# ScalarE weights the gathered rows, VectorE builds plain one-hots, in a two-layer graph kernel

## The reference

```python
h = relu(ln(x @ W1 + b1, g1, bt1))
h_src = h[row]                                   # row = src, col = dst
ef = concatenate([h_src, h[col]], axis=1)
edge_weights = sigmoid(relu(ef @ We1 + be1) @ We2 + be2)[:, 0]
aggr = segment_sum(edge_weights[:, None] * h_src, col, num_segments=n)
gate = sigmoid(concatenate([h, aggr], axis=-1) @ Wg + bg)
h_new = gate * aggr + (1.0 - gate) * h
```

## Time and profile before

| | |
|---|---|
| median of 3 runs | 2092.99 us (2092.58 to 2093.82) |
| profiled execution, its own time | 2085.86 us |
| its span, first to last instruction | 2084.1 us |
| mean granted TensorE clock | 0.898 |

### The profile page before, as it was taken

One profiled execution on the slowest core, in us unless ns is written; L12 is line 12 of the kernel. 1 busy time (PEld: TensorE's weight loads), 2 busy tenths in 40 slices (PEclk: granted clock), 3 DMA queues, 4 the chain that ended last, 5 costly groups with the idle time before them and its releaser, 6 DMA issues.

```text
span 2084.1 us, 44754 instructions
## 1 busy us (share of the span) xinstructions
PE 1614.4 (77%) x14694; PEld 1506.6 (72%) x14695; DVE 1661.9 (80%) x4900; ACT 1087.2 (52%) x2658; POOL 1409.8 (68%) x1430
## 2 busy tenths in 40 slices
PE   4999998766777688887877787887888777787880
PEld 3788786655676677877777787877788777787750
DVE  7777886887998679887888887898797787777766
ACT  1566564676553255554565554565564444444335
POOL 4365530487677777777777777777777777777735
PEclk9999999597888689999999989999899998999995
DMA  7899998037444556655665656666566666666502
GB/s 275 282 333 318 324 366 279 11 101 244 133 140 130 158 161 180 179 175 179 174 179 168 185 175 194 192 187 189 176 205 188 188 188 188 198 176 199 145 18 62
DMA packets 278514, 392.87 MB, mean 189 GB/s; under 512 B 74753, under 2 KB 178436, under 8 KB 278155
## 3 DMA queue, kind: packets, MB, share of 16 engines
q1 hardware_dynamic: 218783, 230.00, 34.7%
q0 software_dynamic: 57024, 155.79, 25.7%
q10 hardware_dynamic: 2476, 4.22, 0.6%
HBM read 374.69 MB, written 15.12 MB: 187 GB/s over the span
## 4 chain that ended last, share of the span: by engine, by line
POOL 46%; PE 20%; issue 18%; DVE 11%; DMA 2%; DVEq 1%; ACT 1%; SPq 0%; ACTq 0%; POOLq 0%
POOL x_rows L969 28%; PE psum L521 10%; POOL ring L969 9%; POOL late_gathers L969 8%; DVE sums L1909 3%; PE psum L1342 2%; PE psum L556 1%; DVE stats L1821 1%; PE psum L1372 1%; PE psum L529 1%; DVE weighted L568 1%; PE psum L573 1%; PE psum L1313 1%; DVE ring L1833 1%; DVE psum L562 1%
## 5 line engine op out<-in xcount | busy, mean ns | idle before, releaser
L969 POOL DMA_INDIRECT x_rows<-src_table,lane_src x720 | 695.8, 966 | 226.4 <-issue 216.4
L562 DVE SCALAR_TENSOR_TENSOR psum<-psum,we_all 128x1024 f32<-128x1024 f32 (+1 forms) x273 | 270.3, 990 | 146.5 <-PE psum L556 145.9
L1179 ACT ACTIVATE weight<-logit,be_all 128x12 f32<-128x12 f32 (+2 forms) x149 | 45.2, 304 | 619.8 <-DVE logit L564 619.8
L556 PE MATMUL psum<-x_rows,ident 128*128 128x128 f32 x1440 | 225.2, 322 | 163.0 <-DMA x_rows<-src_table,lane_src 162.8
L577 DVE TENSOR_TENSOR sums<-sums,psum 128x128 f32 (+4 forms) x812 | 200.9, 247 | 172.5 <-issue 101.0
L556 PEld LDWEIGHTS psum<-x_rows,ident 128*128 128x128 f32 x1440 | 209.5, 231 | 173.0 <-issue 149.1
L564 DVE TENSOR_REDUCE logit<-psum 128x8 f32<-128x1024 f32 (+1 forms) x273 | 266.9, 977 | 20.4 <-issue 0.4
L969 POOL DMA_INDIRECT ring<-src_table,lane_src x236 | 226.8, 961 | 71.9 <-issue 71.9
L969 POOL DMA_INDIRECT late_gathers<-src_table,lane_src x232 | 221.8, 956 | 70.7 <-issue 70.7
L568 DVE TENSOR_SCALAR weighted<-iota,lane_dst,weight 128x40 f32<-128x40 f32 x1188 | 268.9, 322 | 0.0
L521 PE MATMUL psum<-ring 128*64 128x128 f32 x3128 | 221.2, 285 | 24.2 <-issue 19.1
(11 more groups left out here) (266 smaller groups left out, 3406.7 us busy)
## 6 DMA issues: line engine op xcount, KB each, us to landing
ring<-in_edge_attr SPq DMA_DIRECT2D x195, 512.0 KB, 5.4
ring<-rel_table SPq DMA_DIRECT2D x74, 512.0 KB, 5.7
ring<-cell_table SPq DMA_DIRECT2D x121, 256.0 KB
ring<-src_table SPq DMA_DIRECT2D x144, 128.0 KB
x_rows<-src_table,lane_src POOLq DMA_INDIRECT x720
ring<-dst_table SPq DMA_DIRECT2D x297, 32.0 KB
ring<-src_table SPq DMA_DIRECT2D x104, 64.0 KB
src_table<-ring SPq DMA_DIRECT2D x12, 512.0 KB, 2.9
```

Of the source, the lines that this page charges most:

```text
L556: last = eng.matmul(out[:, j, :], ident[:, :], rows_[:, j, 0:P], start=False, stop=True, skip_group_check=True)
L562: eng.scalar_tensor_tensor(hid, hid, 0.0, wide["we2"][:, :].unsqueeze(1).to_broadcast([P, n, P]), ALU.max, ALU.mult)
L969: eng.indirect_dma_start(gathered(c)[:, j, :], None, src_table, bass.IndirectOffsetOnAxis(ap=lane_src[:, t:t + 1], axis=0)).then_inc(gathe ...
```

## The change

ScalarE, behind the sigmoid, drains and multiplies each of the pair's eight gathered h rows (128 x 128 f32) in place by its edge weight; only then is `weight` signalled. VectorE's eight small instructions become one comparison of 128 x 320 elements (`tensor_tensor`, is_equal, both inputs broadcast), which no longer needs the weights and now stands ahead of the rider's instructions; these wait for `weight` where there is a rider. `wsum` waits for `weight` as well. `add_src_part` makes one identity product of 512 columns for a chunk in place of four of 128.

```diff
         def add_src_part(eng, out, rows_):
-            for j in range(J):
-                last = eng.matmul(out[:, j, :], ident[:, :], rows_[:, j, 0:P], start=False, stop=True, skip_group_check=True)
-            return last
+            return eng.matmul(out, ident[:, :], rows_[:, :, 0:P], start=False, stop=True, skip_group_check=True)
...
                 some = slice(0, n * J + (n_cols if n == 2 else 0))
-                eng.activation(weight_[:, some], logit_[:, some], ACT.Sigmoid, bias=be2_all[:, 0:1]).then_inc(done("weight"), 1)
+                eng.activation(weight_[:, some], logit_[:, some], ACT.Sigmoid, bias=be2_all[:, 0:1])
+                eng.drain()
+                for k, c in enumerate(pair_chunks(q)):
+                    for j in range(J):
+                        h_rows = gathered(c)[:, j, P:2 * P]
+                        last = eng.activation(h_rows, h_rows, ACT.Copy, scale=weight[:, q % 4, k, j:j + 1])
+                last.then_inc(done("weight"), 1)
...
             def wsum(q):
                 need(eng, "weigh", q)
+                need(eng, "weight", q)
                 need(eng, "acc2", q - 2)
...
             def weigh_(q):
-                c = SORTED + 2 * q
+                c, n = SORTED + 2 * q, len(pair_chunks(q))
                 need(eng, "wsum", q - 3)
-                need(eng, "weight", q)
+                last = eng.tensor_tensor(weighted[:, q % 3, 0:n, :, :].rearrange("p c j w -> p (c j) w"),
+                                         iota1[:, 0:W].unsqueeze(1).to_broadcast([P, n * J, W]),
+                                         lane_dst[:, c:c + n, :].rearrange("p c j -> p (c j)").unsqueeze(2).to_broadcast([P, n * J, W]), ALU.is_equal)
                 if q in riders:
+                    need(eng, "weight", q)
                     need(eng, "wsum", q - PLACES)
-                    cell_weigh(riders[q], q)
-                for k in range(len(pair_chunks(q))):
-                    last = weigh(eng, weighted[:, q % 3, k, :, :], lane_dst[:, c + k, :], weight[:, q % 4, k, :])
+                    last = cell_weigh(riders[q], q)
                 last.then_inc(done("weigh"), 1)
```

More of the change, by code:

```diff
@@ L1958, in cell_weigh @@
                 for i in range(n):
-                    eng.tensor_scalar(place_dst[u % PLACES][:, i, 0:span(u)], iota_s[:, 0:span(u)], cell[:, 1, at_.start + i:at_.start + i + 1],
-                                      weight[:, q % 4, 2, i:i + 1], ALU.is_equal, ALU.mult)
+                    last = eng.tensor_scalar(place_dst[u % PLACES][:, i, 0:span(u)], iota_s[:, 0:span(u)], cell[:, 1, at_.start + i:at_.start + i + 1],
+                                             weight[:, q % 4, 2, i:i + 1], ALU.is_equal, ALU.mult)
+                return last
             def logits(q):
```

## The result

The changed kernel takes 2106.94 us in the median of 13 runs (2097.07 to 2112.65), the kernel before 2092.99 (13 runs, 2090.86 to 2098.5): ratio 1.0065, 95% interval 1.0054 to 1.0076. It is slower by some 14 us, where I had forecast 2093.2 and a range of 2084 to 2103. Its profiled execution took 2105.29 us with a span of 2103.6, against 2085.86 before; the forecast for it was 2086.1.

A forecast was written before the change was run, and what follows sets the result against it. GpSimd issuing gathers back to back was taken as the bound. The terms -0.9 + 3.9 - 1.7 - 1.1 = +0.2 us gave 2086.1 for the profiled execution, 2093.2 for the median, with a range of 2084 to 2103.

The forecast's parts named there:

- The step that failed: VectorE's added comparison: laid behind each turned one-hot, it would hold 21 gathers for 184 ns on average, +3.9 us.
- the second rival: Slower: a gather held by the turned one-hot is held on until the comparison's end, +20 us, 2113; chance 12%.
- sign of recognition: What would show the second rival: gathers of over 1.45 us by the dozen, gather means of 980 ns and above.
- against: Argument against the second rival: L1959 stands at the same place today, and the gather goes on at L1949's end.
- only five gathers show it: Argument for the faster rival (20%, 2082): 13 instructions like the comparison run beside gathers, and only five gathers show it.
- Eight instructions removed: VectorE's eight 40-column instructions a step: their removal frees the gathers by 0.9 us, ends 0 and 4.9.
- The phase of the turned one-hot: Timing of L1949 to the gathers, deciding 14.9 of today's 20.3 us: taken as 0, 6 us either way.
- ScalarE: Eight added multiplications a step take 2.6 us; ScalarE comes to 8.3 of 10.2 us, hidden.
- The wait for `weight`: `wsum` and the rider's L1959 wait for the multiplications, the rider's up to 1.3 us: no effect on the time.
- The start: Early steps where slots come late: first `wsum` 1 us sooner, later waits vanish, -1.7 us, ends -5.3 and +2.
- The tail: Behind the last gather: `logits` could start 1.1 us earlier, -1.1 us, ends -1.5 and +1.
- TensorE, "nothing": Identity products, 16 instructions in 2.03 us become four in 1.9: 0.15 us of a step where PE isn't the bound.

The follow-up runs named there:

- g1: The changed kernel with its comparison again as eight instructions of 40 columns; 2085.14 us against 2091.82 for the kernel before, ratio 0.996.
- h1: The changed kernel with the comparison as two of 128x160, on a chip paced by PE; 0.9391 of the kernel before.
- h3: The changed kernel with the comparison made twice, a drain between, on a chip paced by PE; 0.9393 of the kernel before.
- i3: The changed kernel with the comparison made twice, a drain between, on another chip paced by PE; 0.9726 of the kernel before.
- f0: The changed kernel once more, unaltered, on a chip paced by PE where the kernel before takes 2525 us; 0.9426 of it.
- g4: The kernel before with the turned one-hot made by four instructions of 256 columns, where gathers are the pace; 0.9978 of the kernel before.

## Why the prediction was wrong

The frame held. GpSimd's gathers were the pace, VectorE's time (183 us less; 194 forecast) and ScalarE's (351 more; 390 forecast) went unseen, and the time was decided by the gathers' own length.

**The step that failed** is the price of the added comparison, "+3.9, ends 0 and 7.4". Its duration was right (484 ns median, 485 forecast), its place too (0.396 us behind the turned one-hot's start). The working laid it beside the gathers and counted those that would start in its own window. What it left out is the second rival, which I gave 12%: gathers that begin in the turned one-hot. I had counted them as going on at its end, as they do in the kernel before with L1959 behind it. Measured, the comparison's own window holds 32 gathers for 7.3 us, the upper end of my range, and the handing on of 51 more adds 19.1 us. That is 26.4 us in place of 3.9. The trace of g1, without the comparison, has 23.9 us less excess, and its time gives 22 us.

The **rival** had the mechanism and the size: "52 × 0.39 = +20 us", measured 51 gathers and 19.1 us. Its sign of recognition came true (22 gathers over 1.45 us, up to 1.75, against one before), its mean of 980 ns as well (981.0). That the time came out at 2107 and not at the rival's 2113 or above is in part luck of the phase: the turned one-hot's own holds fell by 5.9 us, a term that I had put at 0. Why it got 12%: I took from rows 8 that a gather gets in at L1949's end though L1959 has started 0.09 us before. L1959 is a short `tensor_scalar`, the comparison has two tensors as inputs and is long. I had rows with such a short instruction as successor, and none with a two-input one; "against" was an inference from another kind. The same rows had the counter-example: L1909 was still running when the gather came, and L1949 came first. The price also leaned on L1880 alone ("only five gathers show it"): L1865, with two inputs from SBUF as well, had held nine more, 2.5 us, in the same trace.

Term by term:
- *Eight instructions removed:* -0.9 forecast. In the kernel before, none of the 66 gathers that began inside one of them had an excess of 10 ns, and in g1 the eight of one operation hold 0.1 us for certain; the term was of no weight.
- *The phase of the turned one-hot:* 0 with 6 us either way. The turned one-hot's own holds went from 15.4 to 9.5 us, 5.9 less, in the changed kernel, and to 9.5 in g1: just inside the bound.
- *The Trainium skill's* inference ("SBUF — State Buffer", Who interferes with whom) that a `tensor_tensor` doesn't stall the making of a DMA's descriptors, since it takes only the read interface, fails here: 32 + 51 gathers were held until the comparison's end. Its statement that an instruction with two SBUF inputs contends with GpSimd's reads fits, as far as a trace without ports can tell. The turned one-hot held 20 gathers at a later point, 0.83 us behind their start; 28 gathers reached that point with the comparison running and took the median.
- *ScalarE:* eight multiplications take 2.45 us and its sigmoid starts 0.37 ahead of them, 2.8 in all; 151.65 us busy in 200 where I had 163. For the 0.1 us of the drain I had no row; from the sigmoid's end to the first multiplication it is 0.07. The wait at the start of a step vanished as forecast. Held.
- *The wait for `weight`:* PE never waited for it. VectorE's rider instructions wait for the multiplications 57 times, 47.6 us in all, as forecast without effect.
- *The start:* -1.7 forecast. The first wait fell from 4.81 to 4.66 us only; idle time that isn't "issue" is 8.8 us against 10.0. The reason that the rows suggest is that ScalarE works on without pause there, with its sorting behind the multiplications:

```profile
522.82 2.44 ACT L1182 ACTIVATE x_rows<-x_rows,weight 128x128 f32<-128x128 f32 x8
...
525.17 3.58 ACT L1192 ACTIVATE sums<-sums,pos 128x196 bf16<-128x196 bf16 x10
528.82 1.93 ACT L1195 ACTIVATE sums<-sums,ones 128x1960 bf16<-128x1960 bf16 x1
529.19 0.95 POOL L967 DMA_INDIRECT x_rows<-src_table,lane_src  x1 [4.66 <-PE psum L571]
```

  The next slots depend on this sorting; from the multiplications' start to the sorting's end it is 7.9 us, and VectorE's 1.3 us were given to ScalarE. That is argued from the order, not tested. About -1 in place of -1.7.
- *The tail:* -1.1 forecast, -0.5 measured (99.6 to 99.1 us from the last gather to the end).
- *TensorE, "nothing":* not contradicted where gathers are the pace, and untested there. On the PE-paced chips it was the largest term of all.

Sum of the measured terms on the profiled execution: +21.0 in the gathers (17.5 of excess, 3.6 by the median), -0.8 in the idle time between them, -0.3 since the first begins earlier, -0.5 behind them: +19.4, as measured.

## What to carry to other kernels

Where indirect DMAs issued by GpSimd are the pace, look at what runs on VectorE when a gather starts: the `tensor_scalar` of 1024 columns and the two-input instructions from SBUF prolonged it here, those that read PSUM did not, and one directly behind the other they add up. So fewer and longer VectorE instructions can be slower though VectorE's own time falls. The same work in eight short instructions, or a drain in between, let the gather in. And measure on more than one chip before a term is called nothing: the identity products of 512 columns, which I had put at nothing, were worth 2.6% on one visit and 8% on another.

## What the runs showed that I had not expected

- A gather that waits for one VectorE instruction is passed over by a two-input one that follows directly: 51 gathers in the changed kernel, up to 1.75 us. Two halves of 0.32 us pass it on in part (27 gathers to the end of the second in h1, 30 not), and a drain between two comparisons ends it (none of 44 in h3, none of 57 in i3).
- The same kernel took 2086 to 2099 us where gathers are the pace and 2411 to 2543 us on three others, where PE issued single matmuls 0.7 to 1.4 us apart and its granted clock was 0.78 to 0.80. There the changed kernel was faster by 5.7% (f0), against slower by 0.65% where the forecast was made. What pauses PE no row shows.
- Cutting the turned one-hot took 11 us off the gathers' excess and gave back 8 us in waits for slots (377.0 against 369.0 us idle in g4).
